# A quantized gated MLP with generated adapters: unrolled schedule, float16 halves, and a generator spread over 16 steps

## The reference

```
scale = cond @ norm_w.T + 1.0
h = x * (scale[:, None, :] * rsqrt(mean(x * x) + EPS))
val, gate = split(h @ up_w.T, 2)                 # 256 -> 2 x 1024
h = val * gelu(gate)
y = act_quant(h) @ weight_quant(down_w).T        # 1024 -> 256
x = y + x
Wd_b = Wd + (h_lang @ Wdd.T + bdd) * 0.1         # 128 x 256 for each sequence
Wu_b = Wu + (h_lang @ Wdu.T + bdu) * 0.1         # 256 x 128 for each sequence
x = x + relu(x @ Wd_b.T + bd) @ Wu_b.T + bu
```

## Time and profile before

| what | value |
|---|---|
| median of 3 runs (range) | 553.59 us (553.55 to 553.85) |
| span of the profiled execution | 555.9 us (its own time isn't listed) |
| busy TensorE, matmuls | 505.5 us, 91% |
| busy VectorE | 476.0 us, 86% |
| busy ScalarE | 280.4 us, 50% |
| busy GpSimd | 248.8 us, 45% |

### The profile page before, as it was taken

One profiled execution on the slowest core, in us unless ns is written; L12 is line 12 of the kernel. 1 busy time (PEld: TensorE's weight loads), 2 busy tenths in 40 slices (PEclk: granted clock), 3 DMA queues, 4 the chain that ended last, 5 costly groups with the idle time before them and its releaser, 6 DMA issues. The chain is left out here.

```text
span 555.9 us, 11249 instructions
## 1 busy us (share of the span) xinstructions
PE 505.5 (91%) x3206; PEld 393.1 (71%) x3206; DVE 476.0 (86%) x956; ACT 280.4 (50%) x512; POOL 248.8 (45%) x593
## 2 busy tenths in 40 slices
PE   2776867798999999999999999999999999999965
PEld 1655656676777777777777777777777777777732
DVE  4799999999888888888888888888888888888773
ACT  3665674763544445444445444544445545444451
POOL 0363545352444444444444444444444444444491
PEclk9897989788999999999999999999999999999985
DMA  7954767762444444444444444444444444442343
GB/s 259 351 156 159 219 176 168 215 185 56 96 112 99 115 97 104 112 100 100 113 103 112 113 113 113 113 113 113 113 113 113 113 113 108 107 112 68 70 85 132
DMA packets 120377, 71.33 MB, mean 128 GB/s; under 512 B 104672, under 2 KB 105376, under 8 KB 118176
## 3 DMA queue, kind: packets, MB, share of 16 engines
q1 hardware_dynamic: 120352, 71.02, 48.9%
HBM read 37.44 MB, written 8.39 MB: 82 GB/s over the span
## 5 line engine op out<-in xcount | busy, mean ns | idle before, releaser
L597 ACT ACTIVATE gel<-bank,rms 128x512 f32<-128x512 f32 x128 | 87.8, 686 | 210.6 <-PE bank L974 206.5
L974 PE MATMUL bank<-up_hi,xs_hi 128*128 128x512 f32 x512 | 175.1, 423 | 6.6 <-DVE xs_lo L721 6.6
L974 PE MATMUL bank<-up_lo,xs_hi 128*128 128x512 f32 x512 | 163.7, 401 | 0.0
L974 PE MATMUL bank<-up_hi,xs_lo 128*128 128x512 f32 x512 | 163.2, 400 | 0.0
L802 DVE SCALAR_TENSOR_TENSOR hid<-bank,rms,gel 128x512 f32<-128x512 f32 x128 | 95.2, 743 | 45.8 <-ACT gel L597 45.6
L974 PEld LDWEIGHTS bank<-up_lo,xs_hi 128*128 128x128 f32 x512 | 98.0, 191 | 24.1
L974 PEld LDWEIGHTS bank<-up_hi,xs_lo 128*128 128x128 f32 x512 | 97.9, 191 | 24.1
L974 PEld LDWEIGHTS bank<-up_hi,xs_hi 128*128 128x128 f32 x512 | 89.3, 194 | 20.3 <-issue 6.7
L440 POOL TENSOR_TENSOR nwt<-nwt 128x2 f32<-128x2 f32 x96 | 22.1, 231 | 134.7 <-DVE nwt L735 129.6
L828 DVE TENSOR_REDUCE amax<-hid 128x1 f32<-128x1024 f32 x64 | 78.1, 1220 | 2.2
L918 PE MATMUL bank<-tern,qT 128*128 128x256 bf16 x512 | 68.9, 279 | 6.2 <-DMA qT<-qn 4.1
(11 more groups left out here) (89 smaller groups left out, 650.1 us busy)
## 6 DMA issues: line engine op xcount, KB each, us to landing
xT_s<-in_xT SPq DMA_DIRECT2D x32, 256.0 KB, 2.8
xn_s<-in_xn SPq DMA_DIRECT2D x32, 256.0 KB, 3.1
stage<-in_WddT SPq DMA_DIRECT2D x8, 1024.0 KB, 5.2
stage<-in_WduT SPq DMA_DIRECT2D x8, 1024.0 KB, 5.6
out<-out_s SPq DMA_DIRECT2D x28, 256.0 KB, 2.2
adapt<-in_up_wT SPq DMA_DIRECT2D x4, 512.0 KB, 6.6
x<-in_down_wT SPq DMA_DIRECT2D x1, 1024.0 KB, 13.3
qT<-qn SPq DMA_TRANSPOSE x64, 3.2
```

What stands on the lines that cost most here:

```text
L597: nc.scalar.activation(gel[:, c], u_gate[c][:], ACT.Gelu, scale=rms[:, slot, jt % TPB:jt % TPB + 1]).then_inc(gelu_done, 1)
L974: ins = nc.tensor.matmul(dst[:], a[:, (jt // TPB) % 2, k, cols], w[:, c, k, v, :], start=(k == 0 and n == 0), stop=(k == KD - 1 and n == 2))
```

## The change

All loops and lags are replaced by one list of steps s = 0 to 72, written out on every engine.

- `up_hi`, `up_lo`, `xs_hi` and `xs_lo` are float16 instead of float32r, with up_w scaled by 256, which 1/rms takes back.
- The generator has one chunk a step: high and low halves of chunk s in step s, its matmuls in step s+1, its evacuation in step s+2.
- `middle` of sequence b stands in step ADAPT[b], the larger of 2b+10 and 20+(3b+1)//2; the last four in 65, 66, 67 and 69. `output`, `relu` and `middle_low` stand in ADAPT[b]+1.
- The scaled rounding goes from VectorE to ScalarE (`quantize`), one step after the gate, and so does the high half of x (`scaled_high`).
- `down` comes three steps after `up` instead of two. There are two `qn`, three `qT`, 20 `x1` and 3 adapter slots, and no separate buffers for the last sequences.

```
-F32R = mybir.dt.float32r
...
-UP = 2
-QT = UP + 1
-DOWN = UP + 2
-SPLIT_X1 = UP + 5
-XT = SPLIT_X1 + 1
-SPLIT_AD = UP + 9
-MID = SPLIT_AD + 1
-OUT = SPLIT_AD + 2
...
+DOWN = 3
+END = NT + 9
...
+def adapter_step(b):
+    if b >= B - 4:
+        return (NT + 1, NT + 2, NT + 3, NT + 5)[b - B + 4]
+    return max(2 * b + 10, NGEN + 4 + (3 * b + 1) // 2)
+ADAPT = [adapter_step(b) for b in range(B)]
...
+def sequences(s, lead):
+    return [b for b in range(B) if ADAPT[b] - lead == s]
+def split_tiles(s):
+    return [2 * b + i for b in range(B) for i in range(TPB) if ADAPT[b] - 4 + i == s]
...
-        up_hi = sb("up_hi", [P, NC, KD, 2, 512], F32R)
-        up_lo = sb("up_lo", [P, NC, KD, 2, 512], F32R)
+        wsplit = sb("wsplit", [P, 2, 2, CHUNK], F16)
+        up_hi = sb("up_hi", [P, NC, KD, 2, 512], F16)
+        up_lo = sb("up_lo", [P, NC, KD, 2, 512], F16)
...
-        xs_hi = sb("xs_hi", [P, 2, KD, S], F32R)
-        xs_lo = sb("xs_lo", [P, 2, KD, S], F32R)
+        xs_hi = sb("xs_hi", [P, 2, KD, S], F16)
+        xs_lo = sb("xs_lo", [P, 2, KD, S], F16)
...
+            for s in range(END):
+                if 2 <= s + 2 < NGEN:
+                    load_chunk(s + 2)
+                if s % TPB == 0 and s // TPB + 2 < B:
+                    load_x(s // TPB + 2)
+                for t in split_tiles(s - 1):
+                    transpose_x1(t)
+                if 0 <= s - 1 < NT:
+                    transpose_q(s - 1)
+                for b in sequences(s, -3):
+                    store(b)
...
+            for s in range(END):
+                if s < NGEN:
+                    low_part(s)
+                if s % TPB == 1 and s // TPB + 1 < B:
+                    rsqrt(s // TPB + 1)
+                for b in sequences(s, -1):
+                    middle_low(b)
+                for b in sequences(s, 2):
+                    adapter_low(b)
+                for b in sequences(s, 1):
+                    output_bias(b)
...
+            def scaled_high(b):
+                act.wait_ge(scale_ready, 1)
+                act.wait_ge(ld_xT[b % XT_SLOTS], slot_count(b, XT_SLOTS))
+                after(act, u_full, (b - 1) * TPB * NC)
+                for k in range(KD):
+                    nc.scalar.activation(xs_hi[:, b % 2, k], xT_s[:, b % XT_SLOTS, k], ACT.Copy,
+                                         scale=scaleT[:, k, b:b + 1]).then_inc(xs_hi_done, 1)
...
+            def quantize(t):
+                act.wait_ge(qscale_done, t + 1)
+                nc.scalar.activation(hid[:, t % 2], hid[:, t % 2], ACT.Copy, bias=ROUND,
+                                     scale=amax[:, t % AM_SLOTS, 2:3]).then_inc(q_done, 1)
+            def quantized(t):
                 act.wait_ge(q_done, t + 1)
-                after(act, y_full, t - 1)
-                if has(t - 1, NT):
-                    act.wait_ge(qT_done[(jt - 1) % 2], 16 * (it * (TPI // 2) + (jt - 1) // 2 + 1))
-                nc.scalar.activation(qn[:], hid[:, jt % 2], ACT.Copy, bias=-ROUND).then_inc(qn_done, 1)
-            def residual_high(it, j):
-                t, jt = tile_at(it, j, SPLIT_X1), j - SPLIT_X1
-                if not has(t, NT):
-                    return
-                if jt % TPB == 0:
-                    after(act, mid_full, seq_at(it, j, SPLIT_X1) - X1T_SLOTS + 1)
-                if isinstance(t, int) and t >= NT - 4:
-                    act.wait_ge(qn_done, NT)
-                else:
-                    after(act, x1T_done[jt % TPB], it * (16 * XN_SLOTS) + 16 * (jt // TPB))
+                if t >= 2:
+                    act.wait_ge(qT_done[(t - 2) % QT_SLOTS], slot_count(t - 2, QT_SLOTS))
+                nc.scalar.activation(qn[:, t % 2], hid[:, t % 2], ACT.Copy, bias=-ROUND).then_inc(qn_done, 1)
...
+            for s in range(END):
+                if s < NT:
+                    gelu(s, 0)
+                if 0 <= s - 1 < NT:
+                    quantize(s - 1)
+                for t in split_tiles(s):
+                    residual_high(t)
+                if 0 <= s - 1 < NT:
+                    quantized(s - 1)
+                if s < NT:
+                    gelu(s, 1)
+                if s % TPB == 0 and s // TPB + 1 < B:
+                    scaled_high(s // TPB + 1)
+                    squares(s // TPB + 1)
+                if s == 0:
                     act.wait_ge(ld_down, 16)
                     nc.scalar.activation(tern[:].rearrange("p j d -> p (j d)"), raw_down, ACT.Abs,
                                          accum_out=wsum[:, 0:1]).then_inc(absum_ready, 1)
-                if ready[1] is not None:
-                    high_part(ready[1], 1, 16 * (ready[1] // 2 + 1))
-                residual_high(it, j)
-                relu(it, j)
-            act.wait_ge(const_ready, 2)
-            nc.scalar.activation(warm[:], zero[:], ACT.Gelu)
-            for n in range(NC * KD):
-                c, k = n // KD, n % KD
-                act.wait_ge(ld_up[n], 16)
-                nc.scalar.copy(up_part(up_hi, c, k), raw_up[:, c, k]).then_inc(up_hi_ready, 1)
-            for j in range(UP):
-                step(0, j)
-            act.wait_ge(ld_small, 16 * N_SMALL)
-            steps(act, step)
-            late_high(B - 4)
-            at(relu, MID, -10)
-            at(residual_high, SPLIT_X1, -5)
-            late_high(B - 3)
-            at(quantized, QT, -1)
-            at(relu, MID, -8)
-            at(residual_high, SPLIT_X1, -4, -3)
-            late_high(B - 2)
-            at(residual_high, SPLIT_X1, -2)
-            late_high(B - 1)
-            at(residual_high, SPLIT_X1, -1)
-            at(relu, MID, -6)
-            at(relu, MID, -4, -2)
+                if s < NGEN:
+                    high_part(s)
+                for b in sequences(s, -1):
+                    relu(b)
...
+            for s in range(END):
+                if s < NT:
+                    gate(s, 0)
+                if 0 <= s - DOWN < NT:
+                    dequantization(s - DOWN)
+                    residual(s - DOWN)
+                for b in sequences(s, -2):
+                    total(b)
+                if 2 <= s < NGEN + 2:
+                    evacuate(s - 2, 0)
+                    evacuate(s - 2, 1)
+                if s == 1:
+                    ternary()
+                if s % TPB == 0 and s // TPB + 1 < B:
+                    scaled_low(s // TPB + 1)
+                if s % TPB == 1 and s // TPB + 1 < B:
+                    rsqrt_guess(s // TPB + 1)
+                for b in sequences(s, 2):
+                    adapter_high(b)
+                if s < NT:
+                    gate(s, 1)
+                    quant_scale(s)
+                for t in split_tiles(s):
+                    residual_low(t)
+                if s < NGEN:
+                    low_part(s)
...
+            for s in range(END):
+                if s < NT:
+                    if s % TPB == 0:
+                        pe.wait_ge(xs_done, s // TPB + 1)
+                    up(s, 0)
+                if s == 1:
                     pe.wait_ge(const_ready, 5)
                     pe.wait_ge(absum_ready, 1)
                     nc.tensor.matmul(sum_ps, ones[:], wsum[:, 0:1], start=True, stop=True).then_inc(absum_full, 1)
-                down(it, j)
-                early = isinstance(t, int) and t == 0
-                if made[0] is not None and not early:
-                    generate(made[0], 0)
-                if has(t, NT):
-                    up(1)
-                if made[0] is not None and early:
-                    generate(made[0], 0)
-                if made[1] is not None:
-                    generate(made[1], 1)
-                middle(it, j)
-                output(it, j)
-            steps(pe, step)
-            at(middle, MID, -10)
-            at(down, DOWN, -2)
-            at(output, OUT, -10)
-            at(middle, MID, -8)
-            at(output, OUT, -8)
-            at(down, DOWN, -1)
-            at(middle, MID, -6, -4)
-            at(output, OUT, -6)
-            at(middle, MID, -2)
-            at(output, OUT, -4, -2)
+                if 0 <= s - DOWN < NT:
+                    down(s - DOWN)
+                if s < NT:
+                    up(s, 1)
+                if 1 <= s < NGEN + 1:
+                    generate(s - 1)
+                for b in sequences(s, -1):
+                    output(b)
+                for b in sequences(s, 0):
+                    middle(b)
```

More of the change, by code:

```diff
@@ L62 @@
 NGEN = 2 * NGC
-GENERATED = 2 * NBK
+GENERATED = 2 * NGEN
+U_SCALE = 256.0
 W_SCALE = 256.0
@@ L69, with pool_cols @@
 XN_SLOTS = 4
[L70 to L75, removed]
-UP = 2
-QT = UP + 1
-DOWN = UP + 2
-SPLIT_X1 = UP + 5
-XT = SPLIT_X1 + 1
-SPLIT_AD = UP + 9
-MID = SPLIT_AD + 1
-OUT = SPLIT_AD + 2
-LATE = B - 4
-LOADED = 3
+QT_SLOTS = 3
+AM_SLOTS = 8
+X1_SLOTS = 20
+X1N_SLOTS = 4
+X1T_SLOTS = 3
+AD_SLOTS = 3
+OUT_SLOTS = 2
+N_SMALL = 6
+N_NEWTON = 11
+DOWN = 3
[9 more added lines that the diff above has]
```

(36 more changed lines are left out.)

551 lines of the change are left out of this document (165 added, 386 removed).

## The result

The change makes the kernel slower: 806.43 us (806.05 to 807.15, 4 runs) against 553.72 us, a ratio of 1.4548 with an interval of 1.452 to 1.4575. The profiled execution took 806.74 us with a span of 805.0. The forecast was slower, 632 us, with a range to 670. The direction and the first mechanism were right; most of the size was not.

A forecast was written before the change was run, and what follows sets the result against it. TensorE was taken to bound the long middle, VectorE the generator. Stages were summed to end at 41.5, 177.5, 195.5, 493.5 and 607.5 us; a 27.4 us tail gave 635, less 2.3, rounded to 632 us; range 588 to 670.

The forecast's parts named there:

- The start: First tiles: VectorE's evacuation wait and two low-clock generator chunks move behind the third tile, whose up ends at 41.5 us.
- The generator: Steps 3 to 17, one chunk a step, with coupled chains: 132 us plus 4 for clock falls; tile 20 at 195.5 us.
- I take 8.8; bounds 8.3 and 10.5: Microseconds per generator step, from a chain through gelu, high parts, GpSimd, chunk load, late transpose, down and up.
- The wait that the change adds: TensorE stalls before each output, behind up, for gelu, relu and GpSimd's middle_low: 27 times, 95 us in steps 21 to 63.
- The odd stall: TensorE's wait before output in odd steps, where GpSimd has rsqrt ahead of middle_low: 3.1 us, 17 times.
- some 2.5 us behind `up(s,0)`: Estimated start of GpSimd's rsqrt operations in odd steps, after gelu, gate, residual and guess; they end at 5.7 us.
- The even stall: TensorE's wait before output in even steps, with scaled_high and squares between gelu and relu: 4.2 us, 10 times.
- The clock: TensorE's clock falls behind 10 even and 10 odd stalls, 1.4 us each: 28 us; bounds none and 76 us.
- Float16: Up-projection matmuls of 512 columns take 0.216 us instead of 0.233: 0.6 us a tile, 38 us in all.
- Costs nothing: Later down-projection priced at nothing; quantization on ScalarE worth nothing in the middle, hidden behind matmuls except scaled_high before even-step relu.
- The rivals: Five alternatives to the 70% main case: 592 us (16%), 509 us (3%), 501 us (1%), 670 us (5%), 680 us (5%).
- The last one: Rival: clock falls behind all 27 stalls, for two up blocks each, 76 us instead of 28: 680 us, 5%.

The follow-up runs named there:

- e5: Changed kernel with four output slots and early relu, plus rsqrt ahead of low_part on GpSimd in odd steps: 549.77 us.
- e7: Changed kernel with four output slots, early relu, rsqrt ahead of low_part on GpSimd, and transpose_q ahead of the chunk load on SyncE: 516.25 us.
- e2: Changed kernel with relu and middle_low back in the step of middle, still two output slots: 619.37 us.
- e1: Changed kernel with four output slots instead of two and 18 x1 slots instead of 20: 730.48 us.
- e9: Changed kernel with four output slots, plus 34 useless 256-column matmuls on TensorE ahead of the wait before output: 667.45 us.
- e3: Changed kernel with both four output slots and relu and middle_low back in the step of middle: 554.13 us.
- e4: Kernel before the change with float16 halves in the up-projection and nothing else: 532.13 us.

## Why the prediction was right or wrong

**The start, right.** 41.5 us for tile 2, measured 38.9.

**The generator, wrong by 27 us at tile 20.** The step that failed is "I take 8.8; bounds 8.3 and 10.5": it was 10.7. (The upper bound is also misadded: a landing of 8.3 in the same sum gives 10.0.) The transpose chain was there, as told (TensorE waits 3.4 to 4.9 us for `qT`), but the chain through GpSimd was drawn without `rsqrt` behind `low_part`, and e5 to e7 show that loop to be as long. That e7's 8.4 us is near the floor of 8.3, ScalarE's load, is luck: ScalarE is busy 103 of 120 us there, 7.2 us a step, and TensorE 7.8 where 7.3 was priced.

**"The wait that the change adds", right in place, wrong in size.** e2 shows that it was the dearest part: 187 us. In e1, with the store out of the way, the 27 stalls are 113 us of idle where 95 were priced. The odd stall was 4.1 to 5.1 us up to step 50 and 4.47 from step 53 to 61, not 3.1. The term that failed is the start of `rsqrt`, "some 2.5 us behind `up(s,0)`". It began 654.45 - 650.23 = 4.2 us behind (3.5 in some of the steps before 50). The prediction saw that `scaled_low` puts off `gate(s,1)` and checked it only against the next up block, not against VectorE's own next gate, which is ahead of the guess. The even stall, priced at 4.2, was 3.9.

**The clock, mis-sized.** The term "20 x 1.4 = 28 us" measured 63 us in e9: a fall behind every one of the 27 stalls, 2.3 us each where 1.4 was taken. The 1.4 came from a block of the old trace (80.42 to 84.70) whose last pairs are at full clock again, and it left out the slow output ahead of the block.

**The wait not seen.** The part on the added wait lists what is behind TensorE's wait; the same was not asked of GpSimd, where `output_bias` waits for a store that has moved to three steps behind `middle`. e1 puts it at 76 us beside the late relu, e2 to e3 at 65. It is 62 of the 98 us by which steps 21 to 50 missed the forecast, 3 of the 26 of steps 51 to 63, and 10 of the tail's 18. Most of the rest of the tail is the same late relu, in front of the last five outputs: e1's tail takes 35.2 us and e3's 27.7, where 27.4 was forecast. So the 170 us by which the span is over 635 are, in round numbers read from e1, e3 and e9, 75 for the store, 35 for the clock, 27 for the generator, 18 for the longer stalls, 8 for the tail and 7 for float16 and small gaps.

**Float16, half right.** The block was 2.59 us as taken; 0.6 us a tile was 0.45 in e4, since the small matmuls take longer beside it. The Trainium skill's 131 ns for such a matmul in a stream (TensorE: Matmul & The Clock Gate, Back-to-back issue gap) isn't what the runs show: a pair comes every 0.43 us, so one every 0.216, at full clock and with a weight load each.

**"Costs nothing", wrong twice.** Both parts help once the other waits are gone: without the later down-projection, priced at nothing, e7 is 53 us slower, and without quantize on ScalarE, also nothing, 20. Both were judged by load and not by what they let others start.

**The rivals.** None held whole. The last one had the fall behind all 27 stalls, which is what happened, but two blocks each and 76 us for it. Each was one mechanism beside my own; a second wait, on another engine, was in none, and the time came out above all of them.

## What to carry to other kernels

When a schedule is rewritten by steps, list for each engine the waits in its stream with the step in which each is released, and do it for the slot waits (stores, buffers) too, not only for data; a wait on a step that isn't over, or hasn't begun, is the first thing to look for. Where a stage stays at its length after a wait is taken out, look for a second one beside it: here two orders gave 4 and 0 us alone and 38 together. The version with four slots, relu in the step of middle and both orders, 516 us, beats the kernel before by 7%.

## What the runs showed of the hardware

- Useless matmuls in front of a wait made the kernel 63 us faster. In e1 each of 27 stalls, 26 of them of 3.7 to 5.1 us and one of 2.3, was followed by a stretch at the lower clock of 1.2 GHz, which took in most of an up block and often the output ahead of it. In e9, with idles of at most 1.4 us in front of the outputs, the granted clock was 1.00 (2.4 GHz) from 223 to 630 us.
- A low part of 896 columns on VectorE took 1.07 us when GpSimd's part began 0.7 us behind it, and 3.15 us when it began 0.16 us behind GpSimd's part of 1152 columns (118.70, 2.36 us), in the changed kernel:

```profile
118.86 3.15 DVE L500 SCALAR_TENSOR_TENSOR wsplit<-stage,wsplit 128x896 f16<-128x896 f32 x1
133.63 1.07 DVE L500 SCALAR_TENSOR_TENSOR wsplit<-stage,wsplit 128x896 f16<-128x896 f32 x1
```

- A float32r matmul of 512 columns comes every 0.233 us and a float16 one every 0.216, but the eight 256-column matmuls ahead of a block take 0.80 us before float32r and 0.87 before float16.
